# Scores from a stacked high and low part of the keys, and the router's product with x on VectorE

## The reference, cut to what matters

```python
B, T, H, P, E = 8, 512, 256, 64, 3      # batches, tokens, width, context rows, experts
nx = layer_norm(x, gamma, beta)
q, k, v = nx @ Wq, ctx @ Wk, ctx @ Wv
weights = softmax(q @ k.T * H ** -0.5)                  # per batch: [512, 64]
combined = concat([nx, weights @ v, cond broadcast])    # [512, 768]
router_probs = softmax(combined @ router_W + router_b)  # [512, 3]
h = silu(combined @ e_w1 + e_b1)                        # three experts, 512 wide each
routed = sum((h @ e_w2 + e_b2) * router_probs)
g = sigmoid(silu(combined @ gate_w1 + gate_b1) @ gate_w2 + gate_b2)
out = x + g * (routed @ out_w + out_b)
```

## Time and profile before

| | |
|---|---|
| median of 3 runs | 437.24 us (436.63 to 437.91) |
| the profiled execution | 437.53 us |
| its span, first to last instruction | 435.7 us |
| TensorE | 429.8 us busy, 1924 matmuls |
| VectorE | 315.6 us (72%) |
| ScalarE | 243.3 us (56%) |
| GpSimd | 105.1 us (24%) |
| granted TensorE clock, mean | 0.998 |

### The profile page before, as it was taken

The page is one execution under the profiler, slowest core; times in us unless marked ns, Lnnn a source line. Parts: engine busy times, 40 slices in busy tenths (PEclk is TensorE's granted clock), DMA queues, the critical chain, the costliest instruction groups (busy, mean ns, idle before and its releaser), DMA issues.

```text
span 435.7 us, 5749 instructions
## 1 busy us (share of the span) xinstructions
PE 429.8 (99%) x1924; PEld 347.6 (80%) x1924; DVE 315.6 (72%) x588; ACT 243.3 (56%) x378; POOL 105.1 (24%) x95
## 2 busy tenths in 40 slices
PE   8999999999999999999999999999999999999995
PEld 7578878888788878887888878888888878888885
DVE  3778579899887777784677777784677757664366
ACT  3365745868465657464565557464565557455340
POOL 2300321051225032402025032402025022402430
PEclk9999999999999999999999999999999999999999
DMA  8899778118537335632643525632642525132302
GB/s 249 232 207 210 186 186 185 24 54 215 121 92 182 107 63 111 175 65 80 134 106 101 136 61 113 176 69 78 131 103 56 136 60 112 35 63 81 75 0 48
DMA packets 77282, 50.31 MB, mean 115 GB/s; under 512 B 55966, under 2 KB 65734, under 8 KB 77254
## 3 DMA queue, kind: packets, MB, share of 16 engines
q1 hardware_dynamic: 75248, 48.09, 46.0%
q0 software_dynamic: 800, 1.58, 1.2%
q10 hardware_dynamic: 1206, 0.29, 0.3%
HBM read 27.29 MB, written 7.93 MB: 81 GB/s over the span
## 4 chain that ended last, share of the span: by engine, by line
PE 97%; DVE 2%; issue 1%; ACT 0%; DVEq 0%
PE bank L609 39%; PE bank L848 34%; PE bank L833 12%; PE bank L676 2%; PE bank L629 2%; PE bank L718 2%; PE bank L654 1%; PE bank L688 1%; PE bank L633 1%; PE bank L732 1%; DVE work L1387 0%; PE bank L754 0%; PE bank L641 0%; DVE quad L1389 0%; PE bank L726 0%
## 5 line engine op out<-in xcount | busy, mean ns | idle before, releaser
L609 PE MATMUL bank<-nx,w1n 128*128 128x512 f32 x672 | 173.3, 394 | 0.0
L1060 ACT ACTIVATE hf<-bank,zb 128x512 f32<-128x512 f32 x112 | 77.1, 688 | 137.3 <-PE bank L833 135.0
L609 PEld LDWEIGHTS bank<-nx,w1n 128*128 128x128 f32 x672 | 125.9, 188 | 27.9 <-issue 0.5
L848 PE MATMUL bank<-h,w 128*128 128x512 f32 x552 | 141.5, 392 | 0.0
L848 PEld LDWEIGHTS bank<-h,w 128*128 128x128 f32 x552 | 103.6, 188 | 24.0 <-DVE h L1418 0.2
L1418 DVE TENSOR_TENSOR h<-hf,h 128x512 fp32r<-128x512 f32 x111 | 86.3, 782 | 49.3 <-ACT h L1064 47.3
L1064 ACT ACTIVATE h<-bank,zb 128x512 fp32r<-128x512 f32 x111 | 75.7, 682 | 0.0
L833 PE MATMUL bank<-wT,vw 128*128 128x512 f32 x224 | 70.8, 398 | 0.0
L833 PEld LDWEIGHTS bank<-wT,vw 128*128 128x128 f32 x224 | 41.9, 188 | 9.8 <-issue 0.5
L1455 POOL TENSOR_TENSOR xq<-xq,quad 128x512 f32<-128x512 f32 x14 | 19.0, 1383 | 108.5 <-DVE quad L1133 108.5
L1470 POOL TENSOR_TENSOR work<-work 128x512 f32<-128x512 f32 x14 | 18.9, 1350 | 72.6 <-DVE work L1335 59.9
(11 more groups left out here) (155 smaller groups left out, 451.2 us busy)
## 6 DMA issues: line engine op xcount, KB each, us to landing
vw<-vw_pair SPq DMA_DIRECT2D x48, 256.0 KB, 3.7
xn<-in_x_dram SPq DMA_DIRECT2D x8, 512.0 KB, 4.7
p_bc<-prob_dram SPq DMA_DIRECT2D x8, 512.0 KB, 5.4
xq<-in_x_dram SPq DMA_DIRECT2D x32, 128.0 KB, 2.8
out_dram<-xq SPq DMA_DIRECT2D x28, 128.0 KB, 2.8
stage<-in_L_xcond_e_w_dram SPq DMA_DIRECT2D x24, 128.0 KB, 4.0
xhat_dram<-xn SPq DMA_DIRECT2D x6, 512.0 KB, 2.9
quad<-xhat_dram SPq DMA_DIRECT2D x24, 128.0 KB, 2.7
```

Source lines behind the costliest of these rows:

```text
L609: mm = pe.matmul(dst, lhs(a), rhs(c), start=first and i == 0, stop=last and i == n - 1)
L848: mm = pe.matmul(bank[place][:, :], lhs, h_tile(s, a), start=c == 0 and i == 0, stop=c == COUNT[g] - 1 and i == 2)
L1060: act.activation(hf[:, s % 2, :], z, ACT.Silu, bias=zb[:, j, b:b + 1]).then_inc(s_h, 1)
```

## The change

From batch 3 on (`STACK0`), the keys of a batch stand in `qk_pair` as 128 weight columns, 64 high and 64 low. `scores` is then 4 passes: 2 with the 128 columns over high `nx`, which leave the high and low sums in two halves of the bank's partitions, and 2 with the 64 high columns over low `nx`. ScalarE copies the low half to `wfull` (`score_low`), VectorE adds the two halves and goes on as before.

The router's columns for `nx` are gone from these batches. VectorE forms them from x hat instead (`router_sum`): for expert 1 and for expert 2 four fused multiply-and-sum instructions each (one for 128 tokens), with the difference of the router's columns against expert 0, times gamma. They stand at slots 10 and 12 of batch b-2 (`SUM_SLOTS`), behind the slot's other DVE steps, and their elementwise product is written to `nxf` and not read. `router_shift` ("rs", slot 3, ahead of `y_turn`) brings the sums to the router's layout in 4 small instructions. The beta part is summed once (`router_beta`, "rb", batch 1 slot 1).

GpSimd makes the differences in batch 0: it loads the router's rows and beta, broadcast to all partitions, forms two differences and two products with beta, loads gamma, all of it ahead of `gated_pair(0)`, and behind `gated_pair(0)` it multiplies the differences by gamma (`router_gamma`). `x_turn(2)` waits for that, since these rows lie in `nxf`. From batch 4 on `load_x` waits for the sums of the batch before it.

```diff
+    STACK0 = 3
+    SUM_SLOTS = ((), (10, 12)) + (B - 2) * ((10, 12),)
-        qkr = sb("qkr", [PART, 2, KC, B, SC], F32R)
+        qkr = sb("qkr", [PART, 2, KC, STACK0, SC], F32R)
+        qk_pair = sb("qk_pair", [PART, KC, B - STACK0, 2, NP], F32R)
...
-        SECOND_PLAN = {0: ["lg_+"], 1: ["px_+"], 2: ["pr_", "vsplit0"], ...
+        SECOND_PLAN = {0: ["lg_+"], 1: ["px_+", "rb"], 2: ["pr_", "vsplit0"], ...
-        EVEN_PLAN = {2: ["nx"], 5: ["sc"], ...
+        EVEN_PLAN = {2: ["nx"], 3: ["rs"], 5: ["sc"], ...
...
+                if b > STACK0:
+                    sp.wait_ge(s_rsum, (E - 1) * (b - STACK0))
                 sp.dma_start(xn[:, :, :], x[b].rearrange(by_rows, p=PART)).then_inc(s_x, 16)
...
             def scores(b):
                 dst = take(MB[0], (s_lgq, b + 1))
+                if b >= STACK0:
+                    for k in range(KC):
+                        pe.wait_ge(s_nhi, KC * b + k + 1)
+                        pe.matmul(dst[0:2 * NP, :], qk_pair[:, k, b - STACK0, :, :].rearrange("p a n -> p (a n)"),
+                                  nx[:, b % 2, HI, k, :], start=k == 0,
+                                  stop=False, skip_group_check=True)
+                    for k in range(KC):
+                        pe.wait_ge(s_nlo, KC * b + k + 1)
+                        mm = pe.matmul(dst[0:NP, :], qk_pair[:, k, b - STACK0, HI, :], nx[:, b % 2, LO, k, :], start=False,
+                                       stop=k == KC - 1, skip_group_check=True)
+                    mm.then_inc(s_sc, 1)
+                    return
...
+            def score_low(b):
+                act.wait_ge(s_sc, b + 1)
+                act.wait_ge(s_wT, b)
+                act.copy(wfull[:, :], bank[MB[0]][NP:2 * NP, :]).then_inc(s_sclow, 1)
...
-                act.copy(qkr[:, HI, i, :, 0:NP], bank[i][:, :].rearrange("p (b n) -> p b n", b=B)).then_inc(s_pa, 1)
+                src = bank[i][:, :].rearrange("p (b n) -> p b n", b=B)
+                act.copy(qkr[:, HI, i, :, 0:NP], src[:, 0:STACK0, :])
+                act.copy(qk_pair[:, i, :, HI, :], src[:, STACK0:, :]).then_inc(s_pa, 1)
...
             def x_turn(b):
                 dve.wait_ge(*x_turned(b))
+                if b == STACK0 - 1:
+                    dve.wait_ge(s_rset, 2 + E - 1)
...
+                if b >= STACK0:
+                    dve.wait_ge(s_sclow, b - STACK0 + 1)
+                    link(dve.tensor_tensor(wfull[:, :], bank[MB[0]][0:NP, :], wfull[:, :], ALU.add))
+                    link(dve.transpose(soft[:, :], wfull[:, :]))
...
+            def router_beta():
+                dve.wait_ge(s_rset, 2)
+                dve.tensor_reduce(red_beta[:, :], rbeta, AX_X, ALU.add).then_inc(s_rbeta, 1)
+                dve.wait_ge(s_rbeta, 1)
+                link(dve.tensor_tensor(lb_bc[:, STACK0:, 1:E], lb_bc[:, STACK0:, 1:E],
+                                       red_beta[:, :].unsqueeze(1).broadcast_to([PART, B - STACK0, E - 1]), ALU.add))
+            def router_sum(b, e):
+                if e == 0:
+                    dve.wait_ge(s_xhat, b + 1)
+                    dve.wait_ge(s_rset, 2 + E - 1)
+                    dve.wait_ge(s_nhi, KC * b)
+                done = (E - 1) * (b - STACK0) + e + 1
+                for t in range(NT):
+                    ins = dve.tensor_tensor_reduce(prod[:, t, :], xn[:, t, :], rdiff[e], 1.0, 0.0, ALU.mult, ALU.add,
+                                                   red_nx[:, e + 1, t:t + 1])
+                ins.then_inc(s_rsum, 1)
+                dve.wait_ge(s_rsum, done)
+            def router_shift(b):
+                for q in range(QUADS):
+                    rows = slice(q * QROWS, (q + 1) * QROWS)
+                    ins = dve.tensor_tensor(lg_nx[:, q:NJ:QUADS, :], red_nx[rows, :, :].rearrange("p e t -> p t e"),
+                                            lb_bc[rows, b, 0:E].unsqueeze(1).broadcast_to([QROWS, NT, E]), ALU.add)
+                link(ins)
...
+            def load_router_rows():
+                pool.wait_ge(s_nhi, KC * 2)
+                pool.wait_ge(s_nlo, KC * 2)
+                pool.dma_start(prod_flat[:, 0:E * H], router_W[0:H, :].rearrange("h e -> (h e)").partition_broadcast(PART))\
+                    .then_inc(s_rload, 16)
+                pool.dma_start(beta_bc, ln_beta.partition_broadcast(PART)).then_inc(s_rload, 16)
+            def router_differences():
+                pool.wait_ge(s_rload, 2 * 16)
+                pool.wait_ge(s_vwp, NG)
+                pool.wait_ge(s_fold, 2 * E)
+                for e in range(E - 1):
+                    ins = pool.tensor_tensor(rdiff[e], r_raw[:, e + 1, :], r_raw[:, 0, :], ALU.subtract)
+                ins.then_inc(s_rset, 1)
+                pool.wait_ge(s_rset, 1)
+                for e in range(E - 1):
+                    ins = pool.tensor_tensor(rbeta[:, e, :], rdiff[e], beta_bc, ALU.mult)
+                ins.then_inc(s_rset, 1)
+                pool.dma_start(gamma_bc, ln_gamma.partition_broadcast(PART)).then_inc(s_rload, 16)
+            def router_gamma():
+                pool.wait_ge(s_rload, 3 * 16)
+                pool.wait_ge(s_rset, 2)
+                for e in range(E - 1):
+                    pool.tensor_tensor(rdiff[e], rdiff[e], gamma_bc, ALU.mult).then_inc(s_rset, 1)
...
                 if b == 0:
+                    load_router_rows()
+                    router_differences()
                     pool.wait_ge(s_wc, 2)
                 if b + 1 < B:
                     gated_pair(b)
                 else:
                     gated_last(b)
+                if b == 0:
+                    router_gamma()
```

More of the change, by code:

```diff
@@ L158, in build @@
         stage = raw.enter_context(nc.sbuf_tensor("stage", [PART, STAGES, KC, 512], F32))
-        work = raw.enter_context(nc.sbuf_tensor("work", [PART, 5120], F32))
+        work = raw.enter_context(nc.sbuf_tensor("work", [PART, WORK], F32))
         ctx_raw = work[:, 0:1024].rearrange("p (t h) -> p t h", t=4)
@@ L295, in plan @@
                     "nx": ((nxt,), {"act": ["nx_hi"], "dve": ["nx_lo"]}, {}),
-                    "sc": ((nxt,), {}, {"dve": ["score_max"]}),
+                    "sc": ((nxt,), {"act": ["score_low"]} if nxt >= STACK0 else {}, {"dve": ["score_max"]}),
                     "ex": ((nxt,), {"act": ["exp"]}, {}),
@@ L303, in plan @@
                     "rm": ((of,), {}, {"dve": ["router_max"]}),
+                    "rb": ((), {}, {"dve": ["router_beta"]}),
+                    "rs": ((nxt,), {}, {"dve": ["router_shift"]}),
                     "px": ((of,), {"act": ["exp_router"]}, {}),
@@ L328, in plan @@
                 steps.append(("gate_factor", b))
+            sums = []
             if when == "post" and engine == "dve":
+                if b + 2 < B and b + 2 >= STACK0 and j in SUM_SLOTS[b]:
+                    sums.append(("router_sum", b + 2, SUM_SLOTS[b].index(j)))
                 if b == 0 and j in FIRST_NORM:
@@ L340, in plan @@
                     steps.append(("x_turn", 2))
+            steps += sums
             return steps
@@ L640, in logits @@
                 pe.wait_ge(s_vr, b + 1)
-                pe.matmul(bank[MB[0]][0:SC, :], vr[:, :], wT[:, b % 2, :], start=False, stop=True,
+                pe.matmul(bank[MB[0]][0:SC, :], vr[:, :], wT[:, b % 2, :], start=b >= STACK0, stop=True,
                           skip_group_check=True).then_inc(s_lg, 1)
@@ L1260, in _ @@
                      "score_max": score_max, "weights": weights, "w_lo": w_lo, "logit_turn": logit_turn, "router_max": router_max,
-                     "router_prob": router_prob, "pair_lo": pair_lo, "ew_turn": ew_turn, "fold_lo": fold_lo, "w1_lo": w1_lo,
+                     "router_beta": router_beta, "router_sum": router_sum, "router_shift": router_shift, "router_prob": router_prob, "pair_lo": pair_lo, "ew_turn": ew_turn, "fold_lo": fold_lo, "w1_lo": w1_lo,
                      "z_bias": z_bias, "b2_out": b2_out}
```

48 lines of the change are left out of this document (35 added, 13 removed).

## The result

| | before | after |
|---|---|---|
| median | 437.48 us (436.63 to 439.19, 13 runs) | 439.39 us (438.67 to 441.62, 13 runs) |
| ratio | | 1.0046, 95% interval 1.0035 to 1.0058 |
| the profiled execution, its span | 437.53, 435.7 us | 438.98, 437.2 us |

What follows compares the result with a forecast made beforehand. TensorE, busy 99% of the span, was taken as the bound. 437.53 - 2.28 (passes saved) + 1.36 (stall at the turn) = 436.6 us, 436.3 against the median; 436.2 predicted, range 434.9 to 438.4.

Steps and rivals of the forecast that it cites:

- TensorE's part: Scores of five batches: two of six passes go at 0.228 us each, saving 2.28 us; wider weights cost nothing.
- The wider weights and `score_low`: Scores: a 128-column weight load (0.188 us) fits the spacing, ScalarE's 0.61 us copy at slot 5 is hidden; cost nothing.
- The router's work: Turn from batch 0 to batch 1: slips of 0.1, 0.95 and 0.31 us make TensorE lose 1.36 us.
- `router_gamma`: Behind `gated_pair(0)`: two GpSimd products get between VectorE's `normalise(2)` instructions, a slip of 0.95 us, bounds 0 and 1.3.
- `router_beta`: Batch 1 slot 1: 0.9 us on VectorE, of which 0.59 us idle ahead of `x_turn(2)` absorbs part; 0.31 us left.
- GpSimd's loads and differences: Batch 0: four 128x256 operations of about 0.65 us, done by 84; VectorE slips 0.1 us, bounds 0 and 0.5.
- GpSimd is late: Rival, chance 0.05: late rows or slow strided operations delay `gated_pair(0)` past 86.45, adding 1.3 us of contention; 437.5 us.
- The fused instruction: `router_sum` at slots 10 and 12: 0.42 us per instruction, 1.7 us for four, hidden in VectorE's idle time; costs nothing.
- half throughput: Rival, chance 0.07: the `router_sum` instruction takes 0.68 us, stalling 0.44 us per batch with sums; 437.1 to 438.4 us.
- two passes: Rival, sharing 0.10 with any unseen per-batch cost: the `router_sum` instruction takes 0.84 us, stalling 1.7 us a batch; 439.6 to 444.8 us.
- The rival on the other side: Slower case: `router_sum` instruction of two passes and more, 3.4 to 8.6 us in all; chance 0.10 shared with unseen costs.
- Another cost in every batch that I don't see: Catch-all for every batch, no mechanism or size given; chance 0.10 together with the `router_sum` instruction taking two passes and more.

Runs made afterwards that it cites:

- after_place: The changed kernel with `ident` and `lb_bc` allocated ahead of `h`, so `h` to `wT` stand at their old addresses; 436.25 us, 0.997 of before.
- before_shift: The kernel before, same instructions, with `h` to `wT` allocated 640 B lower, where the changed kernel has them; 441.12 us, 1.009 of before.
- stack_place: The changed kernel without the router's x part and its preparation, with `h` to `wT` at their old addresses; 434.94 us, 0.9943 of before.
- stack_only: The changed kernel without the router's x part and its preparation, tensors at the changed kernel's places; 438.39 us, 1.0031 of before.
- no_gamma: The changed kernel without GpSimd's two products with gamma, gamma's load and the waits for them; 438.69 us, 1.0026 of before.
- late_gamma: The changed kernel with `h` to `wT` at their old addresses and gamma's products held back behind `normalise(2)`; 435.19 us, 0.9945 of before.
- matched: As late_gamma, with `nx` 448 B and `wT` 704 B higher, so all three distances to the weights are 0 modulo 512; 436.9 us, 0.9996 of before.
- place_nx: The changed kernel with `ident` and `lb_bc` allocated behind `hf`: `nx` and `wT` at old addresses, `h` 640 B lower; 439.18 us, 1.0032 of before.
- all_up128: As late_gamma, but weights and `h` to `wT` all stand 128 B higher than in the changed kernel; 438.62 us, 1.0022 of before.
- weights_384: As late_gamma, but weights stand 384 B and moving operands 512 B higher than in the changed kernel; 435.35 us, 0.995 of before.
- place_lb: The changed kernel with `lb_bc` alone allocated ahead of `h`, so `h` to `wT` stand 512 B below their old places; 436.22 us, 0.997 of before.
- gamma_rem0: As late_gamma, with `zb` ahead of `h` in place of `ident` and `lb_bc`: `h` at remainder 0 of 512 B; 438.99 us, 1.0033 of before.
- gamma_rem256: As late_gamma, with `cols` ahead of `h` in place of `ident` and `lb_bc`: `h` at remainder 256 of 512 B; 438.78 us, 1.0032 of before.

## Why the prediction was wrong, and where it held

**The step that failed** is in "TensorE's part". It takes the two passes that go at 0.228 us each, says that the wider weights cost nothing, and lets every other pass keep its spacing: the sum subtracts 2.28 us from the profiled time with the other 1914 passes untouched. They weren't. The new sizes of the keys moved `h`, `nx` and `wT` against their weights, and each slot went from 3.213 to 3.250 us: 3.3 us in the pair after and after_place, and 3.9 us in the pair before and before_shift (3.3 without the slow start). My list of what would make the prediction wrong had "if TensorE's spacing changes with the wider weights". The spacing did change, but not by their width: stack_place has the wide weights at 3.213 us a slot. I costed every instruction that the diff touches and none of the allocations; the line that decided was `qkr = sb(...)`.

**Step by step, with the placement restored:**
- The whole: 436.2 forecast, 436.25 measured (after_place). The sum was right for the kernel without the shift; that it is met to 0.1 us is luck, since the parts below are known to some 0.5 us each.
- Two passes of six in five batches, 2.28 us: 2.5 us (stack_place; the interval is 1.9 to 3.0 us).
- The wider weights and `score_low`, nothing: stack_place shows no wait of TensorE for a split at all behind 31 us.
- The router's work, 1.36 us: after_place less stack_place is 0.997 - 0.9943, 1.2 us; the change less stack_only, 0.7 us. Right within what these can tell.
- *`router_gamma`*, 0.95 us: 0.9 us (no_gamma) and 1.1 us (late_gamma against after_place), with `normalise(2)` at 4.23 us where I had forecast 4.3. This agrees with the rule of the Trainium skill (SBUF — State Buffer, Who interferes with whom), and where GpSimd's products stand elsewhere `normalise(2)` is at 3.40 again.
- *`router_beta`*, 0.31 us: not settled, up to 0.7 us by one trace. VectorE lost the idle time ahead of `x_turn(2)` that I had counted on: its transpose (L1173 here, L1125 before) had 0.59 us of idle before it and has none:

```profile
102.97 1.25 DVE L1173 STREAM_TRANSPOSE nxf<-quad 128x1024 f32<-128x1024 f32 x1
```

- *GpSimd's loads and differences*: the forecast had them done by 84, with 0.65 us for each operation. In the changed kernel (idle before in brackets):

```profile
79.70 1.35 POOL L1581 TENSOR_TENSOR rdiff<-nxf 128x256 f32<-128x256 f32 x2 [5.22 <-DMA nxf<-in_L_xcond_ln_beta_dram]
81.13 1.94 POOL L1585 TENSOR_TENSOR nxf<-rdiff,nxf 128x256 f32<-128x256 f32 x2
83.02 0.58 POOL L1587 DMA_DIRECT2D nxf<-in_L_xcond_ln_gamma_dram  x1
86.08 1.64 POOL L1555 TENSOR_TENSOR work<-work 128x512 f32<-128x512 f32 x1 [2.48 <-DVE wfull L1221]
```

  The differences take 0.68 us each and the products with beta 0.97. They end at 83.1, and `gated_pair(0)` is not late: it starts at 86.08, and at 86.45 before. The rival "GpSimd is late" is out.
- *The fused instruction*, 0.42 us: in slots 10 and 12 of batch 2 it takes

```profile
178.31 0.42 DVE L1263 CUSTOM_DVE_ANT_0 nxf<-xn,rdiff 128x256 f32<-128x256 f32 x1
178.66 0.08 DVE L1263 DVE_READ_ACCUMULATOR2_ANT red_nx<- 128x1 f32 x1
178.66 0.42 DVE L1263 CUSTOM_DVE_ANT_0 nxf<-xn,rdiff 128x256 f32<-128x256 f32 x1
...
189.53 0.41 DVE L1263 CUSTOM_DVE_ANT_0 nxf<-xn,rdiff 128x256 f32<-128x256 f32 x1
...
189.98 0.69 DVE L1503 TENSOR_TENSOR h<-hf,h 128x512 fp32r<-128x512 f32 x1
```

  0.42 us, and 0.35 from one to the next with the read of the accumulator beside it. The split of slot 13 ends at 190.67, and the waits of TensorE hold none for it, so the steady batches cost nothing. The rivals of half throughput and of two passes are out. For the second, the recorded bounds are a little off: a stall of 8t - 5.0 us that adds up to 2.3 us is reached at t = 0.68 with five batches and at 0.77 with two, not at 0.70 and 0.78; nothing hangs on it. The Trainium skill's rule on scalar-tensor-tensor forms (Vector Engine (DVE) Microarchitecture Reference, Points that are easy to get wrong) doesn't show in this instruction with two f32 sources, 0.42 us as for a plain one; whether the instruction is of the form that the rule means, no run here shows.

**The rival on the other side** had the right sign, through a mechanism that didn't occur. "Another cost in every batch that I don't see", 0.10 together with it, was the place where the truth lay, without a mechanism. At 439.4 us it came out just below that case (439.6), since 3.3 us of spacing were laid on a gain of 1.3; that the two are close is chance.

**Left open.** What in the chip ties the spacing to this distance; whether its grain is 256 or 512 B; which distance is best for each pair, and whether the places of `h`, `nx` and `wT` against each other count too; and why matched and place_nx change their spacing in mid-kernel. The offsets tried against the places of before are 0, -128, -192 and +64 B for all three at once, -128 for `h` alone, and -64 and -320 for `nx` and `wT` alone. The distances of the gate's weights `gw2` were not varied by themselves. All spacings are read from one execution of each kernel, though kernels with the same distances agree to 0.001 us a slot.

## What to carry to other kernels

Compare the spacing of passes in a stretch that the change doesn't touch; if it differs without a wait and at the same granted clock, restore the places with a pad and time that before judging the idea. Here the change at the old distances and with gamma's products held back takes 435.19 us, 0.9945 of before (0.9929 to 0.996), half a per cent below before and 1% below the change as made.

## What the runs showed of the hardware

- The spacing of 128x512 passes in f32 depends on the distance between the weights and the moving operands in a partition: 3.213, 3.227, 3.240, 3.250 and 3.253 us for 14 passes in batch 7 at six sets of distances, 0.2295 to 0.2324 us a pass. The absolute places (all_up128, weights_384) and a shift of 512 B (place_lb) make no difference that these runs can tell. Two places 256 B apart (gamma_rem0, gamma_rem256) are alike too, so the grain may be 256 B. In the slots compared TensorE has no recorded wait.
- At the same places the spacing can still have two values: 3.240 and 3.227 us a slot in matched, 3.253 and 3.240 in place_nx, each held over many slots.
- The loss with `h` alone moved (place_nx, 0.027 us a slot) is most of the loss with all three (0.037), and 0.024 of it lies at the passes over `h`.
- In the changed kernel the slots alternate between two lengths, 3.254 and 3.246 us (399.78, 403.04, 406.28), and in place_nx between 3.244 and 3.236; in the kernel before each takes 3.213.
- The fused multiply-and-sum of 128x256 with two f32 sources takes as long as a plain two-source instruction of that size, 0.42 us, and 0.35 us from one start to the next; its accumulator is read by an instruction of 0.08 us whose start falls together with that of the next one (178.66).
